# A decoder layer on one core: the first phase's combination of a pair moved behind the 3rd and 4th first-layer products of its period

## The reference

```python
def prep(t):                       # t: [b, s, 16 heads, 16]
    h1 = jnp.tanh(jnp.einsum('bshd,do->bsho', t, w1) + b1)     # first layer, 16 -> 256
    return jnp.einsum('bsho,on->bshn', h1, w2) + b2            # second layer, 256 -> 16
qp, kp = (prep(Q), prep(K))
qc = qp[..., :nq] + 1j * qp[..., nq:]      # kc likewise
q1 = jnp.einsum('bshn,nm->bshm', qc, Hc)   # k1 likewise
qe = jnp.real(jnp.einsum('hcb,bshn->cshn', R, q1))   # R: 2x2 rotations of pairs
qq = jnp.sum(qe ** 2, -1)                  # kk likewise
s = qq[:, :, None, :] * kk[:, None, :, :]
attn = jax.nn.softmax(s / s, axis=2)
out = jnp.einsum('bijh,bjhd->bihd', attn, V)
x = _layernorm(x + (out @ wo + bo))
```

## Time and profile before

| | us |
|---|---|
| median of 3 runs (1549.96 to 1550.51) | 1550.42 |
| span of the profiled execution, first to last instruction | 1550.1 |
| TensorE busy, weight loads apart | 1502.6 (97%) |
| ScalarE busy | 847.5 (55%) |
| VectorE busy | 1139.4 (74%) |
| mean granted TensorE clock | 0.993 |

### The profile page before, as it was taken

One profiled execution on the slowest core, in us unless ns is written; L12 is line 12 of the kernel. 1 busy time (PEld: TensorE's weight loads), 2 busy tenths in 40 slices (PEclk: granted clock), 3 DMA queues, 4 the chain that ended last, 5 costly groups with the idle time before them and its releaser, 6 DMA issues.

```text
span 1550.1 us, 28824 instructions
## 1 busy us (share of the span) xinstructions
PE 1502.6 (97%) x11288; PEld 1065.1 (69%) x11288; DVE 1139.4 (74%) x2305; ACT 847.5 (55%) x1123; POOL 372.8 (24%) x404
## 2 busy tenths in 40 slices
PE   8999999899999999999999999999999999999998
PEld 4333333335566666666656898888989898888887
DVE  6445555548799999999967877777676767777675
ACT  5888889876688888888863421222222221222221
POOL 1000000124556667666453300000000000000000
PEclk9999999999899999999999999999999999999999
DMA  7656665446565666657652100000000000000000
GB/s 153 137 112 117 122 121 103 71 95 113 95 93 88 105 89 98 110 78 96 93 169 69 62 1 15 1 14 1 1 15 1 14 1 15 1 15 1 1 14 14
DMA packets 61576, 97.37 MB, mean 63 GB/s; under 512 B 12461, under 2 KB 29881, under 8 KB 61441
## 3 DMA queue, kind: packets, MB, share of 16 engines
q1 hardware_dynamic: 61312, 95.34, 33.3%
q10 hardware_dynamic: 128, 0.20, 0.0%
HBM read 26.29 MB, written 4.19 MB: 20 GB/s over the span
## 4 chain that ended last, share of the span: by engine, by line
PE 84%; DVE 8%; ACT 3%; SPq 3%; issue 2%; DMA 1%; POOLq 0%; DVEq 0%; POOL 0%; ACTq 0%
PE ps L109 79%; SPq L119 3%; PE ps L1277 2%; DVE NM L1495 2%; ACT H L614 1%; ACT PX L1438 1%; DVE EE L758 1%; PE ps L1239 1%; DVE XC L2106 1%; PE ps L1285 1%; PE ps L1914 0%; DMA ST<-QS 0%; PE ps L1905 0%; PE ps L1209 0%; DVE QS L678 0%
## 5 line engine op out<-in xcount | busy, mean ns | idle before, releaser
L1495 DVE TENSOR_REDUCE NM<-ps 128x4 f32<-128x1024 f32 x256 | 307.5, 1219 | 29.2 <-PE ps L109 27.7
L1438 ACT ACTIVATE PX<-ps 128x1024 f32<-128x1024 f32 x256 | 262.2, 1024 | 80.2 <-PE ps L109 79.0
L614 ACT ACTIVATE H<-ps,b1c 128x1024 f32<-128x1024 f32 x256 | 268.2, 1118 | 48.6 <-PE ps L109 47.0
L2066 ACT ACTIVATE GF<-ps,cols 128x512 f32<-128x512 f32 x128 | 88.2, 689 | 295.7 <-PE ps L109 295.6
L109 PE MATMUL ps<-XC,W_sw_w 128*128 128x512 f32 x768 | 185.8, 393 | 0.0
L2257 DVE CAST GH<-GF 128x512 fp32r<-128x512 f32 x192 | 82.0, 427 | 106.9 <-ACT GF L2066 101.8
L109 PEld LDWEIGHTS ps<-XC,W_sw_w 128*128 128x128 f32 x768 | 140.5, 188 | 28.0
L2365 POOL TENSOR_SCALAR RSc<-AGc 128x4 f32<-128x4 f32 x23 | 6.9, 298 | 599.5 <-DVE AGc L2152 599.5
L109 PE MATMUL ps<-PX,VT 128*32 128x256 f32 x2048 | 138.6, 388 | 0.1
L2259 DVE TENSOR_TENSOR GH<-GF,GH 128x512 fp32r<-128x512 f32 x192 | 133.2, 694 | 6.6
L109 PE MATMUL ps<-KT,QT 48*128 48x512 f32 x512 | 128.1, 498 | 3.7 <-DVE NM L1495 1.8
(11 more groups left out here) (240 smaller groups left out, 2560.3 us busy)
## 6 DMA issues: line engine op xcount, KB each, us to landing
KT<-KS SPq DMA_DIRECT2D x128, 192.0 KB, 4.7
ST<-QS SPq DMA_DIRECT2D x254, 96.0 KB, 2.8
QT<-XSb SPq DMA_DIRECT2D x128, 96.0 KB, 4.2
XT<-in_xT_dram SPq DMA_DIRECT2D x8, 512.0 KB, 4.1
raw_a<-in_x_dram SPq DMA_DIRECT2D x8, 512.0 KB, 4.3
CR<-in_ctxT_dram SPq DMA_DIRECT2D x8, 512.0 KB, 4.7
out_dram<-X SPq DMA_DIRECT2D x7, 512.0 KB, 2.9
R_sw_w<-in_sw_w_dram SPq DMA_DIRECT2D x6, 512.0 KB, 5.5
```

Of the source, the lines that this page charges most:

```text
L614: e.activation(H1[s % 8][:, :, :], PP[s % 3][:, :, :], ACT.Tanh, bias=b1c[:, half:half + 1], scale=1.0).then_inc(act_th, 1)
L1438: e.activation(PX[s % 3][:, :, :, :], PP[2][:, :, :].rearrange("p g (c q) -> p g c q", c=2), ACT.Exp, bias=0.0, scale=0.25).then_inc(act_e ...
L1495: e.tensor_reduce(NM[u % 2][:, qc, :, :, i], PP[qc][:, :, :].rearrange("p g (m k) -> p g m k", m=2), AX.X, ALU.max, negate=True).then_inc( ...
L2066: e.activation(g[:, :], o, f, bias=cols[:, col:col + 1], scale=1.0).then_inc(act_g, 1)
```

## The change

On TensorE, `combine_pairs` of unit n stands no longer between the two halves of the first-layer products of its period but behind all four, ahead of `w2`. On ScalarE, `square` stands behind the fourth tanh of the period instead of the second. It touches the 15 periods J = 5, 9, ..., 61. No instruction is added or dropped, and VectorE, GpSimd and SyncE keep their streams.

```diff
@@ tensor
             at = attend_due(J)
             if at is not None:
                 attend(at)
-            n = due(J, 5, 4, NIT - 1)
-            if n is not None:
-                free[7] = combine_pairs(n, free[7])
             n = due(J, 6, 4, NIT - 1)
             if n is not None and at is None:
                 free[7] = norms(n, free[7])
@@
                     w1(4 * J + r)
             if not J:
                 free[7] = project(*pr, 7, free[7])
+            ready = due(J, 5, 4, NIT - 1)
+            if ready is not None:
+                free[7] = combine_pairs(ready, free[7])
             if 1 <= J < NJ:
                 free[6] = w2(J - 1, free[6])
@@ scalar
-            n = due(J, 5, 4, NIT - 1)
-            if n is not None:
-                square(n)
             if J == SOON:
                 first()
             for s in soon(J):
@@
             for r in range(2, 4):
                 if J < NJ:
                     step(4 * J + r)
+            n = due(J, 5, 4, NIT - 1)
+            if n is not None:
+                square(n)
```

## The result

The median of 18 runs after the change is 1553.75 us (1549.53 to 1557.93), of 18 runs before 1550.47 us: ratio 1.0027, 95% interval 1.0018 to 1.0036. That is +3.3 us. The interval is clear of 1, though the difference is only a quarter of a per cent. Forecast were 1555.7 us and slower by 5.3 us: the side and the mechanism were right, the size was 2 us too large.

What follows compares the result with a forecast made beforehand. The prediction took TensorE's stream and its gaps to bound the kernel. Its terms, +6.5 - 0.66 - 0.05 - 0.48 = +5.3 us, added to 1550.4 gave 1555.7 us, with a range of 1552.3 to 1558.6.

Steps and rivals of the forecast that it cites:

- What bounds: Whole kernel: TensorE's own work is 84% of the chain of waits, so its gaps count; ScalarE isn't far off.
- The EE wait of 0.28 us goes: Periods J = 9 to 53: the combination's 0.28 us wait for VectorE's fourth EE tile disappears behind four products.
- The four products take 2.14 us: Ordinary periods: the fourth product waits for the first tanh, as in period 56; 2.14 us in place of 1.60.
- Per period +0.54 us: Twelve periods J = 9 to 53: each grows by 0.54 us, 6.5 us in all.
- Nothing gives it back: Periods 4n + 6: norms don't wait for the later square, 0.4 us to spare, so the 0.54 us stays.
- J = 5: -0.66: Period 5: EE tile late, combination begins as before, `w2` comes at 46.51 instead of 47.17; ends 0 and -0.66.
- J = 57: -0.05: Period 57: G on ScalarE moves by 0.12 us at most, -0.05 us taken; ends 0 and -0.66.
- J = 61: -0.48: Period 61: without the square ahead, XF and then `w2` start 0.48 us earlier; ends 0 and -0.48.
- The clock: TensorE in phase A: the granted clock stays at 1.00 despite the new wait of about 0.75 us every fourth period.
- Rivals 2: The clock falls in the lengthened periods; one more fall costs 3.4 us, giving 1559.1 us; chance 0.07.
- rival 3: The present clock fall from 308 us, behind period 57, goes: -3.4 us, 1552.3 us, no measurable change; chance 0.08.
- The sum: Whole kernel: +6.5 - 0.66 - 0.05 - 0.48 = +5.3 us, slower by 0.34%; own ends 1554.6 to 1557.4 us.

Runs made afterwards that it cites:

- experiment 5: The changed kernel with the third first-layer product of the 12 ordinary periods made twice; one run, 1553.77 us.
- Experiment 6: The changed kernel with one more first-layer product between combination and second-layer products in the 12 ordinary periods; one run, 1564.02 us.
- experiment 4: The changed kernel with the combination between the third and fourth first-layer product; median 1549.18 us, ratio 0.9975 to the kernel before.
- experiment 9: The kernel before with five repeated first-layer products in period 58, in TensorE's wait for VectorE; 1548.59 against 1552.31 us, ratio 0.9974.
- experiment 10: The changed kernel once more, unaltered, on the same chip as the run of before beside it; median 1554.09 against 1552.31 us, ratio 1.0008.
- experiments 1: The kernel before with combination and square moved only in the 12 ordinary periods J = 9 to 53; median 1555.58 against 1550.87 us, ratio 1.0026.

## Why the prediction was right, and where its size was off

1. *What bounds.* TensorE's stream with ScalarE just behind: right, and experiment 5 shows that TensorE stands still for the tanh.
2. *The EE wait of 0.28 us goes.* Right: no row of the 12 periods shows it any more.
3. *The four products take 2.14 us.* Right to 0.01 us (202.83 to 204.97), and TensorE waits 0.74 us in them for the tanh, 0.75 in period 56.
4. *Per period +0.54 us.* This term was mis-sized: it measured +0.395, so 12 x 0.395 = 4.7 instead of 6.5. The step that failed is the silent one, that the combination (1.00, 1.86) and `w2` (1.86) keep their durations in the new order. In a row of distances from start to start, the neighbours' share is in the number: 0.11 us went from the combination, which has another successor now, and 0.03 from `w2`, which has another predecessor. Experiment 6 puts a first-layer product back between them and both return (0.99 and 1.85). Why the neighbours matter isn't shown.
5. *Nothing gives it back.* Right: J = 10 to 54 take 56.82 us instead of 56.86, and the norms didn't wait for the square. In experiment 4, where the period is 0.63 us shorter (4.23), the norms of J = 42 came 0.33 us later for it, so some 0.3 us was to spare, a little less than the 0.4 that I had worked out.
6. *J = 5: -0.66.* It was -0.8 to -0.9 in two pairs of profiles (6.08 and 6.18 with the change, 6.97 and 6.99 without): the same edge of 0.14 on top, and 0.08 of the first pair is an EE tile that came earlier. But the forecast took the late tile of one profile for a property of the kernel. In the profile of experiment 9, which has the old order there, the tile was early and the period took 5.59 us, less than the 5.72 of the changed kernel in experiment 10: without the long wait there is nothing to gain.
7. *J = 57: -0.05.* It was -0.17. All of it is G, which begins 0.18 us earlier within the period; the bound of 0.12 was too tight, since GpSimd starts a little later than G could (3.07 us behind the period's start, G 3.03). The DMA was the last to arrive, as the GpSimd row had said.
8. *J = 61: -0.48.* -0.49.
9. *The clock.* It did hold at 1.00 in the stretch of the ordinary periods (60 to 300 us), with a wait of 0.74 us in every fourth period, in the profile after and in those of experiments 1, 5 and 10. The Trainium skill, page "TensorE: Matmul & The Clock Gate", section "A second HAM failure mode: psum-queue depth-cycling", warned of this pattern, from a kernel in bf16; no run here shows it for these waits, and the measurement decides. Where TensorE stood still for 2.1 us and soon again for 0.6, the clock did fall, and filling the first took the fall away (experiment 9). Rivals 2 and 3 treated one fall as an event of the change. The one near 310 us stayed, with the old order and the new; the others are rather the noise of this kernel, which come and go at the same few places from run to run.
10. *The sum.* Forecast +5.3; by the rows +3.15, by the runs +3.3. Of the missing 2.15 us, 1.8 is point 4, the rest J = 5 and J = 57. The measured 1553.75 us lies below the forecast's own ends (1554.6 to 1557.4), because these allowed a period 0.04 us and the edge alone was 0.14. It lies in the stated range only since that took in rival 3, a fall of the clock that goes, and this is not what happened: that part was luck. So was the base: the median was taken as 0.3 us above the span, where every run since has it at least 1.7 above its own. It did no harm, since the +5.3 was added to the median.

## What to carry to other kernels

Work that stands between a producer's pieces may be there to cover a buffer's return, so before moving it ask which piece reuses the first one's buffer and how long its reader takes. The best place of those tried was neither the old one, where the work waited itself, nor behind all four pieces, where it covered nothing, but between the third and the fourth, where it covered the other wait and the third piece hid its own. A period of the same kernel that lacks the work is the best measure of the gap. A distance from start to start holds an edge that hangs on the neighbours, so when the order changes take it, where there is one, from a place where the new neighbours already meet. A wait that one profile shows for a DMA or a late tile may not be there in the next. And when single runs scatter by several us, compare stages that repeat to 0.02 us, or spans at equal clock.

## What the hardware showed that I had not expected

- The way from one group of matmuls to the next depends on what the next one is: the combination took 0.89 us to `w2` and 0.99 to 1.00 to first-layer products; `w2` 1.74 us to the norms and 1.86 to first-layer products; the projection 1.50 to the means and 1.59 to first-layer products. A pair of first-layer products took 0.66 us whatever came next.
- The clock falls at a few places, near 20, 40, 310, 390 and 860 us (once at 333), with seven different selections in the ten profiles without added work in period 58, and near the end of the kernel in all; what one of these costs (the time at half clock, halved) was between 1.7 and 5.1 us. The best and the worst clock of the 81 runs of before, 0.998 and 0.985, went with spans of 1543.0 and 1559.0 us, and the correction to equal clock takes the scatter of these 81 spans from 3.5 to 0.9 us (one standard deviation), so most of it goes with the clock.
- Ten matmuls without use, put where TensorE stood still, made the otherwise unchanged kernel 0.26% faster (0.09 to 0.42%) than the runs beside it.
